# Sixth stage of a four-layer gated attention stack: statistics four batches ahead, context columns in four slots, every third weight subtraction on GpSimd

## The reference

```python
def _L3_xattn_ref(Q, K, V):
    dk = Q.shape[1]
    x = jnp.einsum('bdn,bdm->bnm', Q, K) / sqrt(dk)
    score = jax.nn.sigmoid(x)
    out = jnp.einsum('bvn,bnm->bvm', V, score)
    return out
...
x = x + jnp.tanh(g_xattn[3]) * _L3_xattn_ref(_layernorm(x, axis=-1), ctx_2048, ctx_2048)
x = x + jnp.tanh(g_ffn[3]) * _L3_ffn_ref(_layernorm(x, axis=-1), L3_ffn_w12, L3_ffn_w3, ...)
```

## Time and profile before

| | us |
|---|---|
| median of 3 runs | 1257.41 (1252.7 to 1260.26) |
| the profiled execution | 1260.89 |
| its span | 1258.7 |
| granted TensorE clock, mean over the span | 0.939 |
| stage six, first scores to the last x update | 961.6 to 1009.3 |
| share of the span, TensorE, VectorE, ScalarE, GpSimd | 84%, 66%, 43%, 44% |

### The profile page before, as it was taken

How to read it: one execution, slowest core, us unless ns; L and a number is a source line. 1 busy time by engine, 2 the same in 40 slices (tenths; PEclk the granted TensorE clock), 3 DMA queues, 4 the chain that set the end, 5 groups by cost and what they waited for, 6 DMA issues and landing times.

```text
span 1258.7 us, 32458 instructions
## 1 busy us (share of the span) xinstructions
PE 1057.4 (84%) x11709; PEld 826.3 (66%) x11709; DVE 835.3 (66%) x2315; ACT 544.1 (43%) x1130; POOL 551.9 (44%) x1095
## 2 busy tenths in 40 slices
PE   4899898987388288889799899999978799789888
PEld 2576666665377244444577677777756589778888
DVE  3566665665555478887788868787765766555465
ACT  2455555554355267767211033333323444256432
POOL 2444555553787488861212252323233426500351
PEclk8899999999589779999899999999979999989999
DMA  5332333232367645542100000000022601134331
GB/s 186 98 98 78 111 102 104 87 123 88 105 196 212 158 123 144 154 121 83 67 1 1 17 26 27 17 25 17 9 64 75 196 2 64 72 118 152 101 99 62
DMA packets 107982, 112.72 MB, mean 90 GB/s; under 512 B 13132, under 2 KB 96292, under 8 KB 107596
## 3 DMA queue, kind: packets, MB, share of 16 engines
q1 hardware_dynamic: 98732, 88.47, 23.0%
q0 software_dynamic: 8256, 22.08, 5.9%
q10 hardware_dynamic: 864, 0.43, 0.1%
HBM read 66.09 MB, written 44.84 MB: 88 GB/s over the span
## 4 chain that ended last, share of the span: by engine, by line
PE 57%; DVE 18%; issue 9%; DMA 6%; ACT 4%; POOL 3%; SPq 2%; another core or an unknown queue 1%; ACTq 0%; DVEq 0%; POOLq 0%
PE psum L2816 5%; DMA PT<-xs 4%; PE psum L1102 3%; DVE mx L2397 2%; DVE x L2191 2%; DVE mx L872 2%; PE psum L2496 2%; PE psum L1701 2%; PE psum L1702 2%; PE psum L1034 2%; PE psum L1703 2%; PE psum L1065 2%; PE psum L1085 2%; PE psum L1070 2%; PE psum L1036 2%
## 5 line engine op out<-in xcount | busy, mean ns | idle before, releaser
L872 DVE TENSOR_REDUCE mx<-psum 128x6 f32<-128x960 f32 (+3 forms) x80 | 80.7, 1009 | 73.8 <-PE psum L1070 67.9
L775 POOL TENSOR_SCALAR veps<-mv 128x1 f32<-128x1 f32 x112 | 33.7, 301 | 206.3 <-DVE mv L762 148.3
L753 POOL DMA_INDIRECT got<-ys,rows_y x64 | 64.1, 1002 | 121.6 <-DMA ys<-yt 95.6
L959 ACT ACTIVATE PT<-psum 128x1024 f32<-128x1024 f32 x64 | 65.5, 1024 | 73.5 <-PE psum L1090 73.4
L2397 DVE TENSOR_REDUCE mx<-psum 128x4 f32<-128x1024 f32 x64 | 76.9, 1205 | 20.4 <-PE psum L2469 20.4
L2438 ACT ACTIVATE PT<-psum 128x512 f32<-128x512 f32 x128 | 69.5, 594 | 26.8 <-PE psum L2480 22.9
L1701 PE MATMUL psum<-xnTh,w7h 128*128 128x256 f32 x256 | 75.3, 294 | 1.6 <-issue 1.3
L1702 PE MATMUL psum<-xnTl,w7h 128*128 128x256 f32 x256 | 73.3, 286 | 1.0 <-issue 1.0
L1703 PE MATMUL psum<-xnTh,w7l 128*128 128x256 f32 x256 | 73.1, 286 | 0.9 <-issue 0.9
L2816 PE MATMUL psum<-mskp,ident_r 128*128 128x512 f32 x256 | 70.8, 413 | 2.9 <-ACT PT L2765 1.6
L2496 PE MATMUL psum<-PT,arena 128*32 128x256 f32 x1024 | 70.0, 389 | 0.0
(11 more groups left out here) (431 smaller groups left out, 3403.9 us busy)
## 6 DMA issues: line engine op xcount, KB each, us to landing
xs<-qpad SPq DMA_DIRECT2D x34, 512.0 KB, 3.3
PT<-xs SPq DMA_DIRECT2D x78, 128.0 KB, 2.1
ys<-yt SPq DMA_DIRECT2D x78, 128.0 KB, 2.1
ctxT<-in_ctxT SPq DMA_DIRECT2D x48, 128.0 KB
ext<-qscr SPq DMA_DIRECT2D x96, 64.0 KB
arena<-in_w SPq DMA_DIRECT2D x16, 320.0 KB, 2.9
w_raw<-in_w SPq DMA_DIRECT2D x12, 384.0 KB, 3.5
q_parts<-kscr SPq DMA_DIRECT2D x66, 64.0 KB
```

Source lines behind the costliest of these rows:

```text
L753: pool.indirect_dma_start(out=dst[:, t % 4, k], out_offset=None, in_=ys[:], in_offset=bass.IndirectOffsetOnAxis(ap=rows_y[:, t, k:k + 1], ...
L872: V.tensor_reduce(mx0[:, u0:u0 + m].rearrange("p j e -> p e j"), src, axis=AX.X, op=ALU.max, negate=True).then_inc(F("mx").sem, 1)
L959: A.activation(PT[:, 1024 * r:1024 * (r + 1)], bank(6, 2), ACT.Exp).then_inc(F("p").sem, 1)
```

## The change

Three things change in stage six. The statistics of a batch are made four batches ahead instead of three, and xn reads them from four slots. Context columns have four slots, two of them in qpad, a tile of stage four that is free by then; they are asked for four batches ahead, and the w7 load comes behind them in SyncE's turn. The subtraction of batches 1, 4, 7, 10 and 13 goes from VectorE to GpSimd, in a common helper w7_rest that waits for the subtraction of the batch before, on whichever engine that was. GpSimd gets an order written out (s6_pool) in place of the loop.

```diff
@@ s6_sp
             def load(b):
-                sp.dma_start(ctxT[:, b % 2], a["ctxT"][:, b]).then_inc(F(f"ctx_loaded{b % 2}").sem, 16)
+                sp.dma_start(ctx_cols[b % 4], a["ctxT"][:, b]).then_inc(cols_in(b).sem, 16)
...
             for b in range(2, 4):
                 load_rows(b)
                 load_w(b)
+                load(b)
             stage_over(sp, 6)
-            for b in range(NB - 2):
-                if b < NB - 4:
-                    sp.wait_ge(F("s_psum").sem, F("s_psum").at(b, 1))
-                    load_rows(b + 4)
-                    sp.wait_ge(F("w7_low").sem, F("w7_low").at(b, 1))
-                    load_w(b + 4)
+            for b in range(NB - 4):
+                sp.wait_ge(F("s_psum").sem, F("s_psum").at(b, 1))
+                load_rows(b + 4)
                 sp.wait_ge(F("y").sem, F("y").at(b, 1))
-                load(b + 2)
+                load(b + 4)
+                sp.wait_ge(F("w7_low").sem, F("w7_low").at(b, 1))
+                load_w(b + 4)
...
+        def w7_rest(V, eng, b):
+
+            w = slice(b * W7C, (b + 1) * W7C)
+            eng.wait_ge(f[6, "w7_high"].sem, f[6, "w7_high"].at(b, 1))
+            if b > 0:
+                eng.wait_ge(f[6, "w7_low"].sem, f[6, "w7_low"].at(b - 1, 1))
+            V.tensor_tensor(w7l[:, w], w7_raw[b % 4], w7h[:, w].bitcast(F32), ALU.subtract).then_inc(f[6, "w7_low"].sem, 1)
+
+        def s6_pool(pool):
+            rs = rstd_step(6, pool)
+            for b in range(4):
+                rs(b, b)
+            for b in range(NB):
+                if b + 4 < NB:
+                    rs(b + 4, b % 4)
+                if n_stages > 7 and b == NB - 2:
+                    pair_rstd(pool, 0)
+                if b % 3 == 1:
+                    w7_rest(nc.gpsimd, pool, b)
...
             def apply(b):
-                ln_apply(6, dve, b, b % 2, xn[:, b % 2, 0])
-
-            for b in range(2):
+                ln_apply(6, dve, b, b % 4, xn[:, b % 2, 0])
+
+            for b in range(3):
                 ln_stats(6, dve, b, None, b)
             apply(0)
-            ln_stats(6, dve, 2, None, 0)
+            ln_stats(6, dve, 3, None, 3)
             apply(1)
             for b in range(NB):
                 if b < NB - 2:
                     dve.wait_ge(F("s_psum").sem, F("s_psum").at(b, 1))
                     apply(b + 2)
-                if b < NB - 3:
-                    ln_stats(6, dve, b + 3, None, (b + 3) % 2)
+                if b < NB - 4:
+                    ln_stats(6, dve, b + 4, None, b % 4)
                 if n_stages > 7 and b == NB - 2:
                     pair_apply(dve, 0)
-                w = slice(b * W7C, (b + 1) * W7C)
-                dve.wait_ge(F("w7_high").sem, F("w7_high").at(b, 1))
-                nc.vector.tensor_tensor(w7l[:, w], w7_raw[b % 4], w7h[:, w].bitcast(F32), ALU.subtract).then_inc(F("w7_low").sem, 1)
+                if b % 3 != 1:
+                    w7_rest(nc.vector, dve, b)
                 dve.wait_ge(F("y").sem, F("y").at(b, 1))
```

More of the change, by code:

```diff
@@ L429, in bass_program @@
         ff_flags(5)
-        stage_flags(6, LN + [("w7_raw0", 16, 0), ("w7_raw1", 16, 0), ("msk_loaded0", 16, 0), ("msk_loaded1", 16, 0), ("q_stored0", 16, 0), ("q_stored1", 16, 0), ("w7_high", 1, 0), ("w7_low", 1, 0), ("ctx_loaded0", 16, 0), ("ctx_loaded1", 16, 0), ("rows_loaded0", 16, 0), ("rows_loaded1", 16, 0), ("s_psum", 1, 0), ("s", 1, 0), ("y", 1, 0)])
+        stage_flags(6, LN + [("w7_raw0", 16, 0), ("w7_raw1", 16, 0), ("msk_loaded0", 16, 0), ("msk_loaded1", 16, 0), ("q_stored0", 16, 0), ("q_stored1", 16, 0), ("w7_high", 1, 0), ("w7_low", 1, 0), ("ctx_loaded0", 16, 0), ("ctx_loaded1", 16, 0), ("v_loaded0", 16, 0), ("v_loaded1", 16, 0), ("rows_loaded0", 16, 0), ("rows_loaded1", 16, 0), ("s_psum", 1, 0), ("s", 1, 0), ("y", 1, 0)])
         ff_flags(7)
@@ L2916, in bass_program, with cols_in @@
         ROW_SLOTS = ("rows_loaded0", "rows_loaded1", "q_stored0", "q_stored1")
+        CTX_SLOTS = ("ctx_loaded0", "ctx_loaded1", "v_loaded0", "v_loaded1")
+        ctx_more = qpad[:].rearrange("p h w -> p (h w)").rearrange("p (s c t) -> p s c t", s=2, c=NC)
+        ctx_cols = [ctxT[:, 0], ctxT[:, 1], ctx_more[:, 0], ctx_more[:, 1]]
+        def cols_in(b):
+            return f[6, CTX_SLOTS[b % 4]]
         def rows_in(b):
@@ L3008, in s6_pe @@
                     pair_transpose(pe, 0)
-                pe.wait_ge(F(f"ctx_loaded{b % 2}").sem, F(f"ctx_loaded{b % 2}").at(b // 2, 16))
+                pe.wait_ge(cols_in(b).sem, cols_in(b).at(b // 4, 16))
                 pe.wait_ge(F("s").sem, F("s").at(b, 1))
@@ L3012, in s6_pe @@
                 for n in range(2):
-                    t = MM(bank(4 + b % 2)[:, 0:C], ctxT[:, b % 2, n], sgm[:, b % 2, n], start=(n == 0), stop=(n == 1))
+                    t = MM(bank(4 + b % 2)[:, 0:C], ctx_cols[b % 4][:, n], sgm[:, b % 2, n], start=(n == 0), stop=(n == 1))
                 t.then_inc(F("y").sem, 1)
@@ L3193, in _ @@
             for s in range(1, n_stages):
-                if s == 7:
-                    pair_rstd(pool, 0)
                 if s != 4:
@@ L3209, in _ @@
                     s5_pool(pool)
+                elif s == 6:
+                    s6_pool(pool)
                 else:
```

## The result

| | before | the change |
|---|---|---|
| median of 22 runs, us | 1255.23 (1247.25 to 1262.86) | 1251.05 (1247.0 to 1256.1) |
| ratio to before | | 0.9961 (95% interval 0.9945 to 0.9977) |
| span of the profiled execution, us | 1258.7 | 1253.2 |
| first scores to first matmul of stage seven, us | 48.67 | 44.74 |

The change is faster by 4.2 us by the medians and by 0.39% by the ratio, with an interval of 0.23% to 0.55%, which is 2.9 to 6.9 us. That is within the 0.5% that the prediction said could hardly be told from no change, but with this many runs it is told. A gain of 4.15 us was forecast, and a time of 1253.3 us, within 1249.0 to 1259.5. The measured 1251.05 us lies in that range, 2.2 us under the forecast time, because the kernel before itself came to 1255.23 us over 22 runs and not to the 1257.41 of three.

A forecast was written before the change was run, and what follows sets the result against it. The prediction took stage six's loop xn, statistics, veps, rstd, xn (2.75 us a batch) as the bound. Terms +0.4 (start), -2.4 (triples), -2.15 (tail) and 0 (stage's end) gave -4.15 us: 1257.41 to 1253.3 us, range 1249.0 to 1259.5.

The forecast's parts named there:

- The loop through rstd: Stage six: xn, statistics, veps, rstd and xn again, through VectorE and GpSimd, set the period of 2.75 us a batch.
- part 1: Stage six, statistics four batches ahead: leaves VectorE's own 2.24 us and, taken alone, gains 0.51 us a batch.
- The price of GpSimd's subtraction: Stage six: one subtraction takes 1.82 us on GpSimd (bounds 1.28 to 2.37), so VectorE stands still for 1.65 us.
- The triples: Stage six, batches 3 to 11: three batches take 7.53 us instead of 8.25 to 8.37, in all -2.4 us.
- The start: Stage six, batches 0 to 2: moved statistics and the first GpSimd subtraction cost +0.4 us.
- The tail: Stage six, x of batch 11 to x of batch 13: 5.05 us become 2.90, a gain of 2.15 us.
- The stage's end: From x of batch 13 to the first matmul of stage seven: pair_rstd no later, 0 us.
- The clock: Rival: gathered waits of about 1.75 us in stage six's loop lower TensorE's clock, up to 1268 us; chance 0.11.
- The change does nothing: Rival: a transfer or ScalarE already sets stage six's pace, result 1257 us; chance 0.02.
- VectorE hardly waits: Rival: most of stage six's stall goes, transfers bound it at 2.2 us a batch, result 1249.7 us; chance 0.12.
- GpSimd kept off by VectorE: Case of the rival that stage six's wait only moved: a triple takes 8.1 us or more, 1255.5 to 1258; chance 0.17.
- part 3: Stage six, every third subtraction on GpSimd: saves VectorE 0.84 us, costs 1.65 us of stall.

The follow-up runs named there:

- e1: The change with all sixteen subtractions on VectorE; ratio to the kernel before 0.9931, stage six 40.58 us.
- e4: The change with batch 13's subtraction back on VectorE; ratio to the kernel before 0.9955, stage six 44.17 us.
- e8: The change run again, nothing altered; ratio to the kernel before 0.9970, stage six 44.90 us.
- e7: The kernel before with only the four column slots and the loads' order of the change; ratio to the kernel before 1.0009, stage six 47.09 us.
- e2: The kernel before with only the five subtractions moved to GpSimd; ratio to the kernel before 1.0047, stage six 53.34 us.
- e6: The change with statistics three batches ahead again; ratio to the kernel before 1.0027, stage six 51.84 us.
- e3: The change with a separate flag for GpSimd's subtractions, so none waits for the one before; ratio to the kernel before 0.9951, stage six 43.39 us.

## Why the prediction was right

The order of the steps, the price and the stall were right. That the gain came out within 0.1 us of the forecast was luck, as the last terms show.

**The loop through rstd** was what bound the stage, and part 1 opens it: e1 shows VectorE's own period of 2.24 us to 0.02.

**The price of GpSimd's subtraction** was taken as 1.82 us and is 1.81. The stall was worked out as 1.65 us and is 1.64 or 1.65, in four places, as the sum had it. For one term, 0.60 us from GpSimd's rstd to the next instruction, the prediction shows no row; in the change it is 0.59 (971.45 to 972.04). The 1.69 us that the prediction scaled from the Trainium skill, "GPSIMD Engine Reference", section 3.1, was 0.12 us low.

**The triples** were worked out as 7.53 us and are 7.59, 7.60 and 7.95 in x updates. The third holds 0.28 us for which VectorE waited on nothing that the profile shows, at the same batch in e4 and e8. Its cause stays open. The kernel before has one turn of 3.12 us among its turns of 2.75 (x of batch 9 to 10, one batch later), so the change need not have brought it. The nine batches gained 1.97 us; 2.4 was taken.

**The start** cost 0.24 us from the first scores to x of batch 2 (0.43 in e8), and from x of batch 0 to x of batch 2 alone 0.34 us (0.35 in e8). 0.4 was charged.

**The tail** was the weakest term: 5.05 to 2.90 us was forecast, 3.70 came. The step that failed is "with nothing behind it on VectorE until the next pair": xn of batch 15 is held for 1.4 us by the subtraction beside it (e4). The 2.15 us were 1.35. With the subtraction on VectorE the same stretch takes 3.16 us (e1 and e4), twice VectorE's x, xn and subtraction end to end (0.40, 0.31 and 0.87 us in e4), so the hold cost 0.54 us more than the work it took away. Whether the stretch would take 2.90 us with neither, no run shows.

**The stage's end** was taken as unchanged and gained 0.85 us, since the clock did not fall there; in that execution stage seven lost 1.4 us to its own fall. e8, without either, has the same 7.09 us. The change is not needed for it: e7, with the columns alone, has 7.11 us, and e2, behind the same wait of 1.97 us as in the kernel before, 7.10.

In sum the stage gained 3.93 us where 4.15 were forecast, and the medians differ by 4.18: terms missed by up to 0.85 us in both directions and cancelled. Without the 0.85 us of the clock the stage gained 3.1 us, a quarter less than forecast. Both figures lie in the interval of the ratio (2.9 to 6.9 us), so the runs cannot tell them apart, and the agreement to 0.03 us shows nothing more.

**The rivals.** The clock stayed at 1.00 through the loop in the change, whose longest wait of TensorE there was 1.4 us and not 1.75. It stayed there in e6 too, with three waits of 1.66 us in the loop and one of 2.18 behind it. Where the waits grew to 2.31 us, in e2, it fell behind the first of two such waits and not behind the second, and fell again at one of 2.45. The Trainium skill, "TensorE: Matmul & The Clock Gate", section "HAM oscillation", tells of a kernel that loses the clock again at every wait for data. Its waits are longer than any in this loop, and no run here shows a fall at every wait, so the range of 1255 to 1268 us that the prediction read from it had little to rest on. "The change does nothing" and "VectorE hardly waits" are excluded by the four waits. "GpSimd kept off by VectorE" was argued from the order of the flags, which parts the two subtractions but not xn from GpSimd's: in the change it is VectorE's xn that is kept off, once.

The prediction had said that part 3 costs half of what part 1 opens, 0.8 us in three batches. By the loop, parts 1 and 2 are worth 4.8 us in nine batches and part 3 takes back 2.8, 0.95 us in three. What the prediction did not draw from it is that the change without part 3, e1, has the shorter stage, 40.58 us against 44.74.

## What to carry to other kernels

Before work is moved to a slower engine, count the stall at the point where the fast engine needs its result, and not the time that it saves there: here 0.84 us were saved and 1.65 paid. When several things are changed in one stage, run each alone and the others without it; by the stage's time in the profiles this change was a gain of 8 us (0.8 of it the clock's) and a loss of 4, and its total looked like a small success. A loop that passes through a second engine for a tiny result (rstd, two operations of one column) is opened by working a turn further ahead, and the loads that were hidden behind it need their slots in the same step.

## What the runs showed of the hardware

GpSimd's subtraction, 128 x 768 with both inputs in SBUF, held two kinds of VectorE operation that started while it ran. The subtraction with two SBUF inputs lasted 2.43 instead of 0.96 us (e3); xn, a TENSOR_SCALAR on one SBUF tile with a mean and an rstd for each row, lasted 1.80 instead of 0.41 (the change, e2, e6, e8). It worked the other way too: GpSimd's small power operation, 0.57 us alone, took 1.22 us beside a VectorE subtraction, and its own subtraction 2.29 us when VectorE's had begun first (e3). The x update, whose second operand is in PSUM, kept its 0.48 us beside it (e2, at 967.80 us), and so did mv its 0.18 (the change, at 972.12 us, and the like places of e3, e4 and e8). The Trainium skill, "SBUF — State Buffer", section "Who interferes with whom", says that the two engines share a pair of ports that one of them holds for a whole instruction, and names operations with two SBUF inputs and the fast modes of tensor_scalar; the times here agree with it. That xn is among the held ones had not been expected, since at 0.41 us for 256 elements it is no faster than the statistics (0.42 us). That comparison does not settle in which mode xn ran: a TENSOR_SCALAR of the same shape with constants in place of mean and rstd takes 0.29 us in the kernel before (line 1271).
